# Last attention's keys: eight tiles in the merged middle instead of four, from its fifth step; three context slots; their mean square on GpSimd

## The reference

```python
x = x + _L2_xattn_ref(_layernorm(x), ctx, ctx)         # softmax of features, context product
x = x + _L2_ffn_ref(_layernorm(x), router_w, A, B)     # 4 experts of rank 16, top 2
x = x + _L3_xattn_ref(_layernorm(x), ctx, Wq_w, ..., kn_w)
x = x + _L3_ffn_ref(_layernorm(x), weight, bias, centroids, assignments)

def _L3_xattn_ref(text, features, Wq_w, Wq_b, Wk_w, Wk_b, fn_w, qn_w, kn_w):
    features_n = rmsnorm(features, fn_w)
    Q = rmsnorm(einsum('btd,fd->btf', text, Wq_w) + Wq_b, qn_w)
    K = rmsnorm(einsum('bsd,fd->bsf', features_n, Wk_w) + Wk_b, kn_w)
    attn = softmax(einsum('btf,bsf->bts', Q, K) / sqrt(512))
    return einsum('bts,bsf->btf', attn, features_n)
```

## Time and profile before

| what | value |
|---|---|
| three runs | 1512.72, 1513.99, 3684.55 us; median 1513.99 us |
| profiled execution: its time, its span | 1514.85 us, 1513.1 us |
| PE busy; weight loads; DVE; ACT; POOL | 97%; 87%; 68%; 61%; 27% of the span |
| granted TensorE clock, mean | 0.992 |
| chain that ended last | PE 54%, issue 26%, DVE 9%, ACT 6%, POOL 4% |

### The profile page before, as it was taken

One profiled execution on the slowest core, in us unless ns is written; L12 is line 12 of the kernel. 1 busy time (PEld: TensorE's weight loads), 2 busy tenths in 40 slices (PEclk: granted clock), 3 DMA queues, 4 the chain that ended last, 5 costly groups with the idle time before them and its releaser, 6 DMA issues.

```text
span 1513.1 us, 27936 instructions
## 1 busy us (share of the span) xinstructions
PE 1472.1 (97%) x9532; PEld 1316.5 (87%) x9532; DVE 1032.4 (68%) x2449; ACT 926.9 (61%) x3133; POOL 402.4 (27%) x461
## 2 busy tenths in 40 slices
PE   8999999999999999998999999999999999989997
PEld 7999999999999998887888888888888888877885
DVE  7556555655565557886777777777777788767776
ACT  4456455545564555547777777777777774466652
POOL 5112011301130102233232323232323242644431
PEclk9999999999999999999999999999999999989999
DMA  5000100010000100101111110101010101011101
GB/s 219 33 29 29 43 29 29 29 43 29 29 29 29 43 29 27 57 35 43 36 43 42 37 50 29 50 29 50 29 50 29 39 8 67 29 46 37 48 15 60
DMA packets 16115, 62.60 MB, mean 41 GB/s; under 512 B 2228, under 2 KB 3764, under 8 KB 10984
## 3 DMA queue, kind: packets, MB, share of 16 engines
q1 hardware_dynamic: 15976, 60.82, 11.5%
HBM read 58.72 MB, written 2.10 MB: 40 GB/s over the span
## 4 chain that ended last, share of the span: by engine, by line
PE 54%; issue 26%; DVE 9%; ACT 6%; POOL 4%; DMA 0%; SPq 0%; POOLq 0%; ACTq 0%; DVEq 0%
PE psY L958 12%; PE psQ L874 9%; PE psKV L898 7%; PE psSO L843 2%; PE psSO L945 2%; POOL wo L541 2%; PE psTP L859 2%; PE psTP L908 2%; PE psQ L859 1%; PE psQ L799 1%; PE psSO L844 1%; PE psTP L928 1%; PE psKV L814 1%; ACT prob L1487 1%; PE psQ L1245 1%
## 5 line engine op out<-in xcount | busy, mean ns | idle before, releaser
L958 PE MATMUL psY<-wo,oT 128*128 128x512 f32 x1536 | 378.2, 394 | 0.7 <-DVE oT L1943 0.2
L958 PEld LDWEIGHTS psY<-wo,oT 128*128 128x128 f32 x1536 | 278.8, 188 | 56.2 <-POOL wo L541 2.2
L541 POOL TENSOR_TENSOR wo<-stage_o,wo 128x512 fp32r<-128x512 f32 x68 | 87.2, 1313 | 310.3 <-ACT wo L1400 279.6
L1400 ACT ACTIVATE pT<-psTP 64x256 fp32r<-64x256 f32 (+1 forms) x192 | 86.5, 451 | 124.2 <-PE psTP L928 123.4
L1490 ACT ACTIVATE prob<-wide,neg_mx 128x128 f32<-128x128 f32 x256 | 99.7, 391 | 81.5 <-DVE neg_mx L2075 81.5
L1487 ACT ACTIVATE prob<-s_sb,neg_mx 128x64 f32<-128x64 f32 x256 | 85.9, 337 | 94.2 <-DVE neg_mx L2075 94.2
L1943 DVE TENSOR_TENSOR pT<-psTP,pT 64x256 fp32r<-64x256 f32 (+1 forms) x192 | 97.6, 508 | 67.3 <-ACT pT L1400 65.5
L665 POOL TENSOR_TENSOR rms<-ms_eps,minus_half 128x5 f32<-128x5 f32 (+1 forms) x64 | 74.2, 1159 | 230.6 <-DVE ms_eps L2088 229.8
L541 POOL TENSOR_TENSOR wq<-stage_q,wq 128x512 fp32r<-128x512 f32 x42 | 53.9, 1301 | 209.3 <-ACT wq L1400 156.6
L898 PEld LDWEIGHTS psKV<-wkv,arena 128*128 128x128 f32 x768 | 100.3, 190 | 6.8 <-DVE kT L2123 1.8
L874 PE MATMUL psQ<-wq,hT 128*128 128x512 f32 x384 | 103.8, 407 | 0.0
(11 more groups left out here) (329 smaller groups left out, 3489.9 us busy)
## 6 DMA issues: line engine op xcount, KB each, us to landing
stage_o<-in_wo SPq DMA_DIRECT2D x16, 1024.0 KB, 4.8
stage_q<-in_wq SPq DMA_DIRECT2D x15, 1024.0 KB, 5.1
stage_kv<-in_wkv SPq DMA_DIRECT2D x12, 512.0 KB, 3.6
stage_q<-in_ctx SPq DMA_DIRECT2D x16, 256.0 KB, 3.0
stage_o<-in_ctxT SPq DMA_DIRECT2D x2, 1024.0 KB, 4.8
stage_q<-in_base SPq DMA_DIRECT2D x2, 1024.0 KB, 4.9
stage_kv<-in_ctx SPq DMA_DIRECT2D x8, 256.0 KB, 3.0
out<-x_res SPq DMA_DIRECT2D x8, 256.0 KB, 2.2
```

Of the source, the lines that this page charges most:

```text
L541: g.tensor_tensor(dst[LO], stage, dst[HI].bitcast(f32), ALU.subtract).then_inc(ld[done or what + "_lo"], 1)
L958: m = mm(psY[:], oT[:, ol, h, :], wo[:, wl, h, :], start=h == 0 and i == 0, stop=h == HQ - 1 and i == 2)
L1400: copy = lambda o, i: nc.scalar.activation(o, i, ACT.Copy)
```

## The change

All eight key tiles are made in the middle, tile n in step t = n+5 (product) and t = n+6 (norm and transposes), the last norm and transposes still in p = 0 of the last attention. What carries it:

- Products of tiles 0 to 3 go to bank psQ, their transposes to psY, both shared with the norm and the y transposes of the same steps; tiles 4 to 7 take psE and psKT, which tiles 0 to 3 had.
- `k_norm` works in place in `stage_q[:, 3]`, and `prob` is left to the middle's `y_T`. The fourth slot of the context is given up for it: tiles rotate through three, and bias, centroid and the two norm weight loads move ahead of the last two context loads in SP's queue.
- The mean square of the keys (scale and epsilon) moves from DVE to POOL, into `power`.
- On PE the gate product goes ahead of the norm transposes; on DVE `ln_lo` of the norm transposes goes ahead of `value_norm`, and `k_norm` ahead of the gates.
- What the keys need first goes earlier: fourth slice of their weight (`wk_hi(0)`, `low_wk(0)`) from the last feed-forward step and from behind POOL's step 4 to the slice's turn; the reciprocal norms of the features (`ms_f`, `pw_f`) from step 7 to step 1; the two bias rows' low parts from step 6 to step 2 (DVE); the product of the two norm weights (`wide`) from step 8 to step 5 (DVE).
- The last attention loses four products, four transposes and what belongs to them on DVE, ACT and POOL; waits that stood for them go.

```diff
-    k3, k_in = prob, stage_q[:, 3]
+    k3 = k_in = stage_q[:, 3]
+    junk_of_k = oT[:, LO].rearrange("p h c -> p (h c)")
     def k_bank(n):
-        return psE if n < 4 else psKV[:]
+        return psQ[:] if n < 4 else psE
     def kT_bank(n):
-        return psKT if n < 4 else psT
+        return psY[:] if n < 4 else psKT
...
-            if n >= 4:
-                sp.wait_ge(M["e_tr"], n - 3)
-            sp.dma_start(stage_q[:, n % 4], io["ctx"][:, n]).then_inc(ld[f"slot{n % 4}"], 16)
-        load("wkv", stage_kv[:, :, 2 * P:4 * P], halves_of(row_of("bk3")), 31)
...
+            if n >= 3:
+                sp.wait_ge(M["e_tr"], n - 2)
+            sp.dma_start(stage_q[:, n % 3], io["ctx"][:, n]).then_inc(ld[f"slot{n % 3}"], 16)
+            if n == 5:
+                load("wkv", stage_kv[:, :, 2 * P:4 * P], halves_of(row_of("bk3")), 31)
...
         def power(what, n, col):
+            if what == "k":
+                pool.wait_ge(N3["k_sq"], n + 1)
+                need(pool, N3["kn"], n)
+                g.tensor_scalar(small[:, 4:5], small[:, 7:8], 1.0 / D, RMS_EPS3, ALU.mult, ALU.add).then_inc(N3["ms_k"], 1)
...
         def k_product(n):
-            need(pe, N3["k_in"], n)
+            if n < 4:
+                pe.wait_ge(LNS[5]["lo"], ln_at(5, n + 2))
+            elif n == 4:
+                pe.wait_ge(LNS[6]["lo"], ln_at(6, 1))
+            else:
+                pe.wait_ge(N3["k_in"], n)
...
         def k_transpose(n):
             pe.wait_ge(N3["kn"], n + 1)
-            need(pe, N3["kT_lo"], n)
+            if n < 4:
+                pe.wait_ge(M["x_add"], n + 4)
...
         def middle_step(t):
-            s, f, e, n = M, FF[2], t - 5, t - 9
+            s, f, e, n = M, FF[2], t - 5, t - 5
...
+            if 0 <= e < NT:
+                gate_product(f, e)
             if 0 <= t - 4 < NT:
...
                 ln_transpose(5, t - 4, free)
-            if 0 <= e < NT:
-                if t == NT:
-                    value_product(t - 2)
-                gate_product(f, e)
...
-            if 4 <= t < 7:
-                wk_hi(t - 3)
+            if 4 <= t < 8:
+                wk_hi((t - 3) % KT)
...
-            if t == NT + 2:
-                act.wait_ge(FS["experts"], 2 * NT)
-                wk_hi(0)
...
             if 0 <= n - 1 < NT:
                 k_norm(n - 1)
-            if 5 <= t < NT:
-                eT_lo(t)
-            if t == NT:
-                value_norm(t - 2)
             if 0 <= e < NT:
                 gates(f, e)
-            if 0 <= t - 2 < NT and t != NT:
+            if 0 <= t - 4 < NT and t > 4:
+                ln_lo(5, t - 4)
+            if 0 <= n - 1 < 4:
+                kT_lo(n - 1)
+            if 0 <= t - 2 < NT:
                 value_norm(t - 2)
...
-            if t == 6:
+            if t == 2:
                 dve.wait_ge(ld["vec_hi"], 1)
...
-                if p < 4:
-                    if p == 0:
-                        pe.wait_ge(FS["x_add"], 3 * NT)
-                    k_product(p + 4)
```

100 lines of the change are left out of this document (40 added, 60 removed).

## The result

The changed kernel takes 1521.20 us (median of 14 runs, 1519.06 to 1524.23), the kernel before 1515.14 us (median of 14 runs beside them). The ratio is 1.0044, with a 95% interval of 1.0037 to 1.0051: 6.1 us slower by the medians. The ratio is over the fast runs alone, without one of 3684.55 us among before's 14, and makes it 6.7 us. That is within 2%, but the time is 0.2 us outside the range of the forecast, and the difference more than twice the +2.7 us of the sum.

The account below looks back on a forecast made before the run. PE was taken to fill the last attention, handover chains over DVE and ACT to bound the middle. Terms -0.3 + 10.8 - 9.2 + 1.4 = +2.7 us gave 1517.5 profiled, forecast 1516.7 as median; range 1508.5 to 1521.

Parts of the forecast that it names:

- Steps 5 to 9 of the middle: Where the early key tiles are added; claimed to make the last of these steps' key products end 10.8 us later.
- K to K: From one moment when PE begins what follows a key product to the next such moment, one middle step later.
- The two ways: Chains between key products: through PE and the key transposes, 11.2 us; through ACT, gates and `ln_lo`, 11.15 in step 7.
- K9: Moment PE begins what follows step 9's key product; forecast 1386.9 against 1376.12 before, 10.8 us later.
- The clock: Step 8 of the middle: a fall to 1.2 GHz before the key product costs 2.8 us; half taken, 1.4.
- The last attention: Four products and four transposes leave it, 13.0 us of PE work; claimed gain 9.2 us.
- p = 3 loses a product and a transpose (3.2): Last attention: 3.2 us of PE work go, but similarity(0) waits 0.5 to 0.8 for its norm's low part.
- The lower bound of 7: Last attention: least gain, 7 us, if every removed product's cover of waits was worth 1.5 us.
- The small moves: Weight copy, bias rows and other work moved within the middle's early steps; claimed net -0.3 us.
- slower: Rival: low clock takes hold around step 8's product, step 9 and another wait; 1519 to 1523 us, chance 0.15.
- Bound by PE's own work: Faster rival: PE's own work sets the middle, last key product only 4.1 us later; 1508.6 us, chance 0.22.
- The ports: Rival: `k_norm` on DVE overlaps POOL's low part of `kvs`, up to 0.46 us in steps 6 to 8; 1518.1, chance 0.10.

Follow-up runs that it names:

- a_trlate: Changed kernel with PE transposing the keys of tiles 0 to 3 behind the step's value and context products instead of ahead: 1518.96 us, ratio 1.0033.
- a_sq4: Changed kernel with ACT's squares of the keys of tiles 0 to 3 on 4 columns instead of 512: 1519.21 us, ratio 1.0035.
- a_bias3: Changed kernel with the two bias rows' low parts on DVE at the end of step 3 instead of step 2: 1519.96 us, ratio 1.0034.
- a_comb: Changed kernel with bias rows in step 3, key transposes behind the context product, POOL's dense slices a place earlier: 1522.20 us, ratio 1.0054.
- a_prod3: Changed kernel with 3 matmuls instead of 12 in the key products of tiles 0 to 3: 1517.75 us, ratio 1.0022.
- a_lowshift: Changed kernel with POOL's low parts of dense weight slices 1 to 3 one place earlier in the last attention: 1520.87 us, ratio 1.0041.
- b_small: Kernel before with the change's small moves alone, bias rows in step 2, no key tile moved: 1512.10 us, ratio 0.9985.
- b_fill7: b_small3 plus 7 thrown-away matmuls of 512 columns on PE ahead of the wait that ends step 7: 1511.71 us, ratio 0.9981.
- b_small3: Kernel before with the change's small moves, but bias rows' low parts at the end of step 3, no key tile moved: 1512.58 us, ratio 0.9988.
- b_bias3: Kernel before with only the two bias rows' low parts moved, from step 6 to the end of step 3: 1512.55 us, ratio 0.9989.

## Why the prediction was off

- **Steps 5 to 9 of the middle: right.** Forecast 11.2, 11.15 and 11.35 from K to K in steps 6 to 8 and 9.0 in step 9; measured 11.29, 11.20, 13.02 (of which 1.6 is the clock) and 8.90. The waits of 1.3 us ahead of the key transposes and of 2.4 behind the value product of step 8 are there (1.27 and 2.42). The two ways (a_trlate) and the squares as a link of both (a_sq4) are shown. K9 is 12.0 us later counted from the first mark, forecast 11.9 with the small moves and the clock.
- **The clock: right in kind, its size in part luck.** I took 1.4, half of 2.8 for want of a reason to choose, and it was 1.6, at the product and behind the wait named. Behind the same wait other traces paid nothing (a_sq4) or 2.5 (5.49 us instead of 3.0 in a_bias3 and a_comb). What I had not seen is that the low stretches move with every edit of a chain (a_prod3, a_comb), so that terms worked out at 2.4 GHz do not add up.
- **The last attention, the step that failed: 9.2 forecast, 7.35 measured.** Counted from `q_proj(0)`, `q_proj(2)` came 3.2 us nearer (3.3 forecast), `attend(0)` 5.75 (5.1), and the scores of p = 4 6.8 (8.0). Up to p = 2 the walk had been too careful; the miss lies in "p = 3 loses a product and a transpose (3.2)" and in "p = 4 and 5 lose a transpose each and about 0.3 of waits: 9.2 in all". The product's cover was worth more than the similarity's wait (0.71, as forecast): PE also waits 1.43 us for `normalise`, which POOL holds up, and in p = 4 0.51. I had priced this contention for `k_norm` in the middle, where it came to 0.16 us each in steps 6 and 7 (0.91 us against 0.75 in steps 9 to 12) and to nothing in step 8, and not for the pair of operations that the removal would bring side by side. With that pair apart (a_lowshift) the term is 8.5; for the last 0.7 no cause is shown beyond the features op of p = 2. The lower bound of 7 for the term was the better guide.
- **The small moves: wrong by themselves, right in the sum.** Alone they are worth 2 us (b_small) and not 0.3. But that gain is the end of step 7's wait, and the changed kernel has another chain there. Against a kernel with the small moves alone the early tiles cost 8 to 9 us.
- **What I summed against.** The forecast was tied to the median of three runs, 1513.99; beside the changed kernel before's was 1515.14. This is 1.15 us of the miss of 4.5, the last attention 1.85, the middle 0.6 (12.5 against 11.9, since the profiled execution of before had lost 0.8 us more to the clock than two others). Some 0.9 us (1.5 by the ratio) isn't found in the two traces. Further low stretches like the one at 1419.5 would be of that size; that they are the cause is argued, not shown.
- **The rivals.** The case that came true is the one that I had called slower, with 0.15: its time holds (1519 to 1523), its reason only in part, since the clock took 1.6 us and not 2.8 or more. Bound by PE's own work: refuted by the 6.4 us of idle PE in three steps. The ports: 0.16 us each in two steps and not 0.46 in three. The forecast had set the 1.72 us of the features op against `k_read`, which reads PSUM; the better measure is the same op alone, 0.75 us (at 1428.76 above).

The change moved 13 us of PE's work out of a place where it cost 7.4 into one where it costs 12.5. Both are chains: a product in series with a loop costs nearly its whole length (taking out 2.1 us gave 1.8 in the second stretch of a_prod3), unless it covers another wait (0.8 in the third); a product beside a loop costs only what the loop can't hide.

## What to carry to other kernels

Price a removal by what PE would wait for next, and look for pairs of DVE and POOL operations that come to lie side by side once the product between them is gone. Price an addition by whether it stands in series with the handovers, not by the idle share of the engine. And before any chain is shortened in a stretch with waits, look at the granted clock: here three quarters of four products taken out (a_prod3) gave 3.4 of their 8.4 us back. Whether thrown-away matmuls in the waits are a remedy stays open: they gave 0.9 us at most (b_fill7 against b_small3), within the scatter. And one trace is not enough for a statement on the clock: look at the same wait in several kernels first.

## What was unexpected of the hardware

- With work taken out the clock was lower: 0.75, 0.97, 1.00 and 0.65 over the four steps of a_prod3's one trace against 1.00, 1.00, 1.00 and 0.84, and 0.992 against 0.994 as the mean of all its executions.
- The same wait brings the clock down in one trace and not in another: 1.78 us at the end of step 7 (it fell in b_small and b_small3, not in b_bias3), 2.42 us ahead of the fourth key product (not in a_sq4), 2.14 us in the last attention (in three traces of eleven).
- A DVE operation of 0.29 us on 128 columns took 1.25 us beside a POOL subtraction and ended with it; with the subtraction moved away it took 0.29 us again. Two one-row subtractions took 2.40 us instead of 1.39 where a POOL subtraction lay beside them and ended 0.55 us behind it. Which engine is held turned on 0.1 us in the start (features and their low part, p = 2).
- Over executions whose computing code is the same up to there, the first mark lies between 1305.90 and 1311.14 us. A difference of a few us between two profiled executions has to be cut at marks before it is explained.
